# Two transformer layers on one core: the first layer's layer-norm transposes, projections and output products move to other beats

## The reference, cut to what matters

```
h = layernorm(x) * (1 + ca) + sa
q, k, v = h @ Wq + bq, h @ Wk + bk, h @ Wv + bv     # 16 heads of 8 channels
scores = q k^T / sqrt(8), masked above the diagonal
w = softmax(scores)
x = x + ga * (concat(w v) @ Wo + bo)
```

## Time and profile before

| | |
|---|---|
| median of 3 runs | 1027.99 us (1027.54 to 1029.23) |
| the profiled execution | 1028.94 us, span 1027.2 us, mean granted TensorE clock 0.981 |
| busy share of the span | PE 91%, DVE 76%, ACT 73%, POOL 53% |
| first attention | from about 30 to 313 us of the span |
| one exponential, ACT L872, 128x512 | 597 ns mean |
| reductions on DVE | 1216 ns (L944), 1085 ns (L947), 950 ns (L951) |

### The profile page before, as it was taken

The page is one execution under the profiler, slowest core; times in us unless marked ns, Lnnn a source line. Parts: engine busy times, 40 slices in busy tenths (PEclk is TensorE's granted clock), DMA queues, the critical chain, the costliest instruction groups (busy, mean ns, idle before and its releaser), DMA issues. The chain is left out here.

```text
span 1027.2 us, 23002 instructions
## 1 busy us (share of the span) xinstructions
PE 931.0 (91%) x8664; PEld 513.0 (50%) x8664; DVE 776.5 (76%) x1319; ACT 747.8 (73%) x1380; POOL 541.3 (53%) x755
## 2 busy tenths in 40 slices
PE   4789989889888999999999799999999999989896
PEld 3234343343436888888888533333333333333575
DVE  4778878878864776767777678979788898994476
ACT  2388878878786566666665488888888888889663
POOL 4376766677632121322111078687777869666343
PEclk8599999999999999999999999999999999999999
DMA  7323332221104522425233021211202021100011
GB/s 181 96 74 121 114 104 78 74 76 50 51 26 124 167 82 74 114 90 148 61 106 96 20 84 30 59 35 53 75 14 77 13 84 35 56 13 14 25 32 52
DMA packets 63598, 73.91 MB, mean 72 GB/s; under 512 B 14136, under 2 KB 46008, under 8 KB 63104
## 3 DMA queue, kind: packets, MB, share of 16 engines
q1 hardware_dynamic: 62336, 69.23, 23.5%
q10 hardware_dynamic: 1152, 3.21, 1.0%
HBM read 39.24 MB, written 2.77 MB: 41 GB/s over the span
## 5 line engine op out<-in xcount | busy, mean ns | idle before, releaser
L872 ACT ACTIVATE at_E<-at_Sb 128x512 f32<-128x512 f32 x832 | 440.9, 597 | 75.7 <-PE at_Sb L718 70.2
L944 DVE TENSOR_REDUCE mx<-at_Mb 128x2 f32<-128x1024 f32 x242 | 280.6, 1216 | 40.3 <-PE at_Mb L681 39.1
L718 PE MATMUL at_Sb<-QP,KP 64*128 64x512 bf16 (+3 forms) x1024 | 202.3, 342 | 16.7 <-ACT full_k L419 7.1
L766 PE MATMUL at_Ob<-at_E,VP 128*32 128x256 f32 (+2 forms) x2816 | 204.5, 371 | 2.2 <-POOL at_E L1046 1.0
L1046 POOL TENSOR_TENSOR at_E<-at_E,factor 128x512 f32<-128x512 f32 x128 | 162.3, 1273 | 65.3 <-ACT at_E L872 55.7
L681 PE MATMUL at_Mb<-KP,QP 62*128 62x512 bf16 x996 | 169.7, 348 | 8.5 <-DVE mx L944 6.5
L947 DVE TENSOR_REDUCE mx<-at_Mb 128x2 f32<-128x768 f32 (+1 forms) x128 | 136.7, 1085 | 52.9 <-PE at_Mb L681 51.8
L1057 POOL TENSOR_SCALAR_AFFINE_SELECT at_E<-at_E 128x512 f32<-128x512 f32 x128 | 80.0, 645 | 71.8 <-ACT at_E L872 71.8
L718 PEld LDWEIGHTS at_Sb<-QP,KP 64*128 64x128 bf16 x1024 | 73.5, 95 | 82.6 <-ACT at_E L872 37.9
L766 PEld LDWEIGHTS at_Ob<-at_E,VP 128*32 128x32 f32 x2816 | 58.2, 108 | 88.1 <-issue 65.6
L1498 DVE TENSOR_TENSOR ex_hh<-ex_R,ex_th 128x512 f32<-128x512 f32 x88 | 64.6, 734 | 49.4 <-ACT ex_th L1435 48.7
(11 more groups left out here) (213 smaller groups left out, 1441.8 us busy)
## 6 DMA issues: line engine op xcount, KB each, us to landing
QP<-q SPq DMA_DIRECT2D x96, 128.0 KB, 2.4
KP<-k SPq DMA_DIRECT2D x91, 128.0 KB, 2.4
ex_R<-rw_dram SPq DMA_DIRECT2D x32, 256.0 KB, 3.5
ctxN<-Oev SPq DMA_DIRECT2D x16, 256.0 KB, 2.5
denB<-rdram SPq DMA_DIRECT2D x64, 64.0 KB
ex_R<-rw_dram SPq DMA_DIRECT2D x16, 224.0 KB, 3.5
ex_R<-rw_dram SPq DMA_DIRECT2D x16, 192.0 KB, 3.3
ex_R<-rw_dram SPq DMA_DIRECT2D x16, 160.0 KB, 2.8
```

Of the source, the lines that this page charges most:

```text
L718: return pe.matmul(out[:, at:at + SEQ - q0], KP[p0:p0 + ROWS_H, b % 2, 2 * g + a, kt * P:(kt + 1) * P], QP[p0:p0 + ROWS_H, b % 2, 2 * g + ...
L766: last = pe.matmul(Ob[VW * i:VW * (i + 1), 0, q0:q1], weights_of(b, G, kt, i, q0), moving, start=(kt == 0 and q0 == 0), stop=False, skip_g ...
L872: nc.scalar.activation(dst, src, ACT.Exp).then_inc(s["s_read"], 1)
L944: v.tensor_reduce(mx[:, G % 2, :, t % 2, t // 2], src, AX.X, ALU.max).then_inc(s["m_read"], 1)
```

## The change

Only the first attention is changed. The table of beats is now:

| | LN | q | k | v | recip | ctx | out | weights | stats | aggregate | powers | normalise | split q | split k |
|---|---|---|---|---|---|---|---|---|---|---|---|---|---|---|
| before | 14 | 17 | 20 | 6 | 9 | 17 | 19 | 21 | 7 | 8 | 10 | 11 | 19 | 27 (3 of the next) |
| after | 10 | 15 | 21 | 3 | 6 | 14 | 16 | 19 | 2 | 3 | 4 | 5 | 16 | 22 |

All PE work of the table now stands in positions 3 and 4 of a group, and the output product comes last in its beat. The early k of batch 1 goes from beat 5 to 4, the router's product `elog` from beat 20 to 21 of batch 6.

```diff
-            (14, 17, 20, 6, 9, 17, 19) if causal else (24, 26, 28, 8, 10, 20, 22))
-        WEIGHTS_AT = 21 if causal else OUT_AT + 3
+            (10, 15, 21, 3, 6, 14, 16) if causal else (24, 26, 28, 8, 10, 20, 22))
+        WEIGHTS_AT = 19 if causal else OUT_AT + 3
...
-        EARLY = {0: "ln", 2: "q", 5: "k"} if causal else {0: "ln", 3: "q", 6: "k"}
+        EARLY = {0: "ln", 2: "q", 4: "k"} if causal else {0: "ln", 3: "q", 6: "k"}
...
-                if causal and out_of(beat) is not None:
-                    out_proj(out_of(beat))
...
-                if not causal and out_of(beat) is not None:
+                if out_of(beat) is not None:
                     out_proj(out_of(beat))
...
-                if at == (LN_AT - 7 if causal else 13) and 2 <= n + 2 <= last_b:
+                if at == (2 if causal else 13) and 2 <= n + 2 <= last_b:
...
-                if at == (LN_AT - 6 if causal else 16) and 2 <= n + 2 <= last_b:
+                if at == (3 if causal else 16) and 2 <= n + 2 <= last_b:
...
-                if at == LN_AT - 4 and 2 <= n + 2 <= last_b:
+                if at == (4 if causal else LN_AT - 4) and 2 <= n + 2 <= last_b:
...
-                if at == LN_AT - 3 and 2 <= n + 2 <= last_b:
+                if at == (5 if causal else LN_AT - 3) and 2 <= n + 2 <= last_b:
...
-                if at == Q_AT + (2 if causal else 1) and FIRST <= n + 2 <= last_b:
+                if at == Q_AT + 1 and FIRST <= n + 2 <= last_b:
                     split("q", n + 2)
-                if not causal and at == K_AT + 1 and FIRST <= n + 2 <= last_b:
+                if at == K_AT + 1 and FIRST <= n + 2 <= last_b:
                     split("k", n + 2)
-                if causal and at == 3 and FIRST <= n + 1 <= last_b:
-                    split("k", n + 1)
```

More of the change, by code:

```diff
@@ L564, in attention_phase @@
         END = BEATS + OEV_AT - BPG + 1
-        NEXT_FILLS = {(6, 16): "eln", (6, 20): "elog", (7, 10): "erw"} if causal else {(6, 20): "sln"}
-        EARLY = {0: "ln", 2: "q", 5: "k"} if causal else {0: "ln", 3: "q", 6: "k"}
+        NEXT_FILLS = {(6, 16): "eln", (6, 21): "elog", (7, 10): "erw"} if causal else {(6, 20): "sln"}
+        EARLY = {0: "ln", 2: "q", 4: "k"} if causal else {0: "ln", 3: "q", 6: "k"}
         FIRST = 2
```

## The result

The changed kernel took 1041.79 us (median of 4 runs, 1040.29 to 1043.09), the kernel before 1028.61 us on the same chip (1027.54 to 1029.49). The ratio is 1.0125, 95% interval 1.011 to 1.014: slower by 13 us. The forecast was 1034.1, with a range to 1040. The direction was right; the size said, 6.1 us, was a little under half of the 13.2 that came, and the time lies outside the range. The profiled execution took 1040.29 us (span 1038.6), against 1028.94 (span 1027.2) for the one of before.

A forecast was written before the change was run, and what follows sets the result against it. PE's own work was taken as the bound, with only 2.4 us of waits per regular batch to win. Batch terms 3.1 + 0.1 + 5.3 + 0.1 - 2.0 - 0.5 gave +6.1 us: 1034.1 against the median, range 1023.5 to 1040.

The forecast's parts named there:

- Regular batch: First layer: pieces between mask matmuls become 8.1, 7.1, 8.7 and 8.6 us; batch 32.5 us, a change of -0.7.
- Rival A: POOL finishes splits before PE needs the shifts, so idle beats absorb the fills; faster, 1023.5 us; chance 0.25.
- denB in batches 1 and 3: Broadcast denominators land 1 us late beside the expert weight load, 0.8 reaching PE; +0.1 us for each batch.
- Batch 2: DVE's L323 waits 6.0 us for denominators behind the gates load; PE idles 5.5, clock costs 1.7; +5.3 us.
- Batch 0: Reciprocal root and normalisation behind k's split on POOL delay beat 8's mask matmul to 59.0; +3.1 us, bounds 0 and +5.
- Batch 5: v comes ahead of the wait on L987, which still holds POOL's chain from P2 to P8 (9.1 us); -2.0 us.
- Batches 4, 6, 7: L983 behind the context in 4, experts' normalisation in 6, few maxima in 7; together -0.5 us, bounds -2 and +2.
- Rival C: Denominators late in every batch; batches 1, 3, 4, 5 and 6 pay 1 us each; 1039 us; chance 0.15.

The follow-up runs named there:

- the kernel with three edits: Changed kernel with expert weight loads at beat 18, gates' load behind the denominators, first batch's powers and normalise at beats 7 and 8; 1025.15 us.
- the run that held the clock: Changed kernel plus 16 idle matmuls on PE ahead of its wait for POOL at beat 8 of batch 0; 1042.05 us.
- the run with the reciprocal at 9: The kernel with three edits, with the reciprocal of the denominators put back from beat 6 to beat 9; 1028.38 us.
- the run with the gates behind: Changed kernel with batch 2's gates load issued behind the denominators' load and the rows that follow it; 1037.75 us.

## Why the prediction was wrong in size

**Regular batch: right.** Predicted pieces 8.1, 7.1, 8.7 and 8.6; measured 8.15, 7.02, 8.57 and 8.55 (in the changed kernel the third piece is free of the wait for denB only in batch 5; the kernel with three edits has 8.57, 8.64 and 8.58 in batches 1 to 3). The sum is 32.3 where 32.5 was said. k's split on POOL ahead of the shifts decides P20 to P2 as forecast: L662 waits 1.1 us for POOL there in all six batches. q's does not decide P14 to P20: the sign that the prediction named for it, L662 waiting in most batches, is seen only in batch 0, which has no output product (1.10 us), and slightly in 4 and 6. PE's own 8.7 set that piece, so the number held without POOL. Rival A (POOL gets through in time) is refuted: with k's split out of the way or shortened, P20 to P2 lost 0.9 to 1.1 us.

**denB in batches 1 and 3: the step that failed.** The term that was mis-sized is the lateness of denB beside the expert weights' load: I took 1 us from bounds of 0 and 4.7, "of which 0.8 reach PE", and booked +0.1 for each. The sign that I had for it, four issues in 3.22 us and not 2.8, was none: with the load moved away they took 3.22 and 3.46. Landing came 2.8 us late in batch 1 (wait of 3.01 where 0.2 was due) and 1.8 in batch 3. I also gave these waits no clock: in batch 1 PE idled 3.46 us and then ran about 3 us at 0.50. Measured +4.2 and +0.9, together 4.8 over the forecast. With the upper bound of 4.7 us of lateness, reaching PE in full, the sum would have come to about 1041.5, an estimate from 1034.1 and twice 3.7. The weights' load at another beat removes both, so the cause is shown. The trace of before held the hint: the same load was issued beside denB (92.30 and 92.34), and only three more beats of DVE work hid when it landed.

**Batch 2: mechanism right, size a little high.** Wait 4.49 for about 6, PE idle 4.16 for 5.5, clock at 0.50 for a little over 3 us, 3.4 forecast. +3.6 for +5.3. The gates' load does only half of it: without it the wait was 2.16, with both loads out of the way 0.49. The weights' load is the rest, which the prediction did not name for this batch.

**Batch 0: mechanism right.** P8 at 59.94 for 59.0, chain in the order that was written: split, reciprocal root, normalisation, clearing, shifts at 57.64. The wait of 4.46 brought a clock fall that I had not counted, 1.6 us by the run that held the clock. +4.4 for +3.1.

**Batch 5** gave 2.3 for 2.0, in part by luck. P2 to P8 is 9.80 for 9.1, and what holds it is not POOL's chain but DVE: PE is idle 1.97 us for the maxima behind L985 (L987 before), and L662 waits for ACT (0.70). The clock fall of the earlier trace rows is gone here, but five later kernels whose idle stretch at this place is 1.96 or 1.97 us too had it again (10.4 to 10.6 us from P2 to P8). The row in the changed kernel, and the clock behind the like row of the kernel with three edits (219.92, idle 1.97):

```profile
234.36 0.28 PE L701 MATMUL at_Mb<-maskk,maskq 64*128 64x256 bf16 x2 [1.97 <-DVE mx L945]
```

```profile
221.00:224.00 3.00, 3.00 (x26) 0.85 (x22) 2.20 (x4) 1.74 (x4) 2.92 (x9) 0.58 0.30 86
```

**Batches 4, 6, 7**: -1.0 for -0.5; in 7 the reciprocal ahead of two reductions lost about 1 us of clock, and the run with the reciprocal at 9 (idle 1.42 us there, where it was 1.65) has no such fall.

Sum over the first layer: +6.1 said, +9.8 measured in the profiled executions: batches 1 and 3 +4.8, batch 0 +1.3, batch 2 -1.7, the rest -0.8. The medians differ by 13.2, the profiles by 11.35; I leave the 1.8 between them to the spread of executions and did not test it. Rival C, denB late in every batch, was nearest with 1039, but by luck: batches 4 and 6 do not wait and batch 5 waits 0.16.

**The clock, by the skill's rule.** The prediction priced batch 2's clock with the Trainium skill, "TensorE: Matmul & The Clock Gate", section "HAM oscillation — how this bites in real kernels": the throttled time times one minus the clock ratio. Batch 0 tests it: from 58.5 to 62.6 PE had some 4 us at 0.50, so the rule says about 2, and holding the clock saved 1.6. The rule was a fair upper bound here, and it should have been applied to every long wait and not to batch 2 alone.

## What to carry to other kernels

Before an operation that waits for a DMA is moved earlier, find when the transfer lands and not only when its consumer used to run; a consumer that never waited hides this, and then the upper bound belongs into the range. List every other transfer that is under way between its issue and its landing (here some 5 us), on any queue; one with slack can move instead, and three such moves of loads and of POOL work turned a loss of 13 us into a gain of 4, and with k's split later into one of 8.6. Price each new idle stretch of PE, here from 1.65 us on, with its clock behind it. And don't price a bundle as the sum of its parts: the normalisation alone lost 8.5 us, though it is part of a bundle whose regular batch is 0.9 us shorter.

## What the runs showed of the hardware

- The four broadcast loads of denB were usable 5.0 us behind their first issue in batch 1 of the kernel with three edits, where no load of weights or gates was under way (93.67 to 98.67), and 7.0 and 7.7 us behind it where an expert weight load was issued 1.3 and 1.1 us later on another engine's queue. The queues were apart, and still the one load delayed the other (DMA engines 0.77 busy in 98 to 102). A load that was issued earlier did no such harm: in batch 2 of the changed kernel it took 4.7 us (137.44 to 142.14), with the weights' load, issued 3.3 us ahead of it, still on the DMA engines (0.98 busy in 137 to 138).
- Whether the clock falls behind an idle stretch of PE is not settled by its length in these rows: 1.65 us in batch 7 of the changed kernel and 1.70 us in batch 2 of the run with the gates behind were followed by 0.50, 1.71 us in batch 3 of the changed kernel was not. Batch 5 has one long idle stretch, ahead of L701, in all twelve kernels that contain the change: of 1.96 or 1.97 us in nine, where the clock stayed at 1.00 in four (the changed kernel among them) and fell in five; of 2.5 us in three, where it fell in one. Neither outcome should be read as what an edit did.
- Five kernels with the same code up to batch 0's beat 8 left the starting clock of 0.50 in the windows that begin at 41 (twice), 42, 49 and 51 us, and had it again behind the wait there, twice for some 7 us and three times for some 10. P8 to P14 of batch 0 was 8.0 and 8.5 in the two, 10.1 to 10.3 in the three. It may be a part of why executions of one kernel spread (1024.5 to 1035.7 for the one with the context back); that was not tested.
- VectorE's multiplication L323 took 1.64 us in batch 1 of the changed kernel, beside POOL's L432, and 0.69 in the kernel with three edits, without it; L432 took the 1.15 that it takes anywhere, but POOL's next instruction, L434, took 0.94 for 0.62:

```profile
103.27 1.15 POOL L432 TENSOR_TENSOR full_q<-full_q,q 128x512 f32<-128x512 f32 x1
```

The Trainium skill, "SBUF — State Buffer", section "SBUF: two separate sides", has VectorE with two SBUF inputs and GpSimd take turns at a shared port. The trace agrees: L432 started 0.05 us ahead and ran 1.10 us beside the multiplication, which is 0.95 us longer; L434 then started while the multiplication was still at work and is 0.32 us longer. Here both engines wait, each when it comes second.
